# Steps 14 and 15 of a gated cross-attention kernel in a new order, with roundings, masks and weight loads moved

## The reference

```
x = x + tanh(g_xattn) * attention(layernorm(x), ctx, ctx)     # 16 heads of 16 channels, biases, output projection
x = x + tanh(g_ffn)   * moe(layernorm(x))

moe: t = rmsnorm(x) * norm_w
     probs = softmax(t @ gate_w.T); the two best of 8 experts, weights renormalised
     h1 = t @ w1.T + 2 * (t @ a1[e].T) @ b1[e].T ;  h3 likewise with w3, a3, b3      # F = 1024, rank 16
     act = silu(h1) * h3
     out_e = act @ w2.T + 2 * (act @ a2[e].T) @ b2[e].T ;  out = weighted sum of the two
```

## Time and profile before

| | |
|---|---|
| median of 3 runs | 507.66 us (506.61 to 508.35) |
| profiled execution, its own time | 509.6 us |
| its span, first to last instruction | 507.7 us |
| mean granted TensorE clock | 0.993 |
| TensorE busy | 487.7 us (96%) |
| VectorE busy | 357.9 us (70%) |
| ScalarE busy | 266.6 us (53%) |
| GpSimd busy | 282.4 us (56%) |

### The profile page before, as it was taken

One profiled execution on the slowest core, in us unless ns is written; L12 is line 12 of the kernel. 1 busy time (PEld: TensorE's weight loads), 2 busy tenths in 40 slices (PEclk: granted clock), 3 DMA queues, 4 the chain that ended last, 5 costly groups with the idle time before them and its releaser, 6 DMA issues.

```text
span 507.7 us, 11754 instructions
## 1 busy us (share of the span) xinstructions
PE 487.7 (96%) x4350; PEld 456.2 (90%) x4350; DVE 357.9 (70%) x768; ACT 266.6 (53%) x584; POOL 282.4 (56%) x339
## 2 busy tenths in 40 slices
PE   7888999999999999999899999999999999999996
PEld 6657999999999999997789999899999999999994
DVE  6866777877878877888577869856486456854444
ACT  4456766666676777667666533443335333233331
POOL 5645666666666666561676536644386444854440
PEclk9989999999999999999989999999999999999999
DMA  7793786677777777553601000010000100001001
GB/s 199 180 289 93 216 214 153 157 182 190 189 179 180 180 176 169 120 111 57 204 10 17 1 0 1 1 34 0 1 0 2 34 1 1 0 2 34 0 1 32
DMA packets 51144, 45.83 MB, mean 90 GB/s; under 512 B 33935, under 2 KB 40115, under 8 KB 51088
## 3 DMA queue, kind: packets, MB, share of 16 engines
q1 hardware_dynamic: 41310, 23.18, 19.6%
q0 software_dynamic: 7504, 18.69, 14.1%
q10 hardware_dynamic: 2274, 3.21, 2.0%
HBM read 20.59 MB, written 6.66 MB: 54 GB/s over the span
## 4 chain that ended last, share of the span: by engine, by line
PE 84%; DVE 6%; DMA 5%; issue 2%; ACT 2%; POOL 1%; ACTq 0%; DVEq 0%
PE bank L1368 14%; PE bank L1223 7%; PE bank L1246 7%; PE bank L1372 7%; PE bank L1385 6%; PE bank L1420 6%; PE bank L1205 6%; PE bank L1259 6%; PE bank L1193 5%; PE bank L1400 4%; DMA QS<-crow 3%; PE bank L1292 3%; PE bank L1403 2%; PE bank L1180 2%; PE bank L1335 2%
## 5 line engine op out<-in xcount | busy, mean ns | idle before, releaser
L970 DVE TENSOR_REDUCE nmax<-bank 100x1 f32<-100x361 f32 x256 | 130.0, 529 | 38.4 <-PE bank L1223 33.4
L419 POOL TENSOR_TENSOR awl<-hb,awh 128x400 fp32r<-128x400 f32 x63 | 70.2, 1114 | 109.4 <-ACT awh L627 109.4
L529 ACT ACTIVATE pt<-bank 120x400 f32<-120x400 f32 (+1 forms) x192 | 90.3, 503 | 25.8 <-PE bank L1246 12.2
L627 ACT ACTIVATE awh<-hb 128x400 fp32r<-128x400 f32 x64 | 34.5, 539 | 119.0 <-DVE hb L906 118.7
L1223 PE MATMUL bank<-KS,QS 96*100 96x362 f32 x256 | 86.9, 358 | 5.2 <-DVE nmax L970 4.8
L899 DVE TENSOR_TENSOR hb<-sil,bank 128x400 f32<-128x400 f32 x64 | 36.5, 570 | 73.7 <-PE bank L1385 37.9
L1246 PE MATMUL bank<-QS,KS 97*120 97x200 f32 (+1 forms) x384 | 66.4, 271 | 1.6 <-ACT pt L529 1.0
L1246 PEld LDWEIGHTS bank<-QS,KS 97*120 97x120 f32 (+1 forms) x384 | 60.2, 184 | 2.8 <-DMA QS<-crow 1.7
L328 POOL TENSOR_TENSOR cth<-craw,cth 128x724 fp32r<-128x724 f32 x16 | 27.7, 1729 | 63.0 <-ACT cth L475 54.8
L1223 PEld LDWEIGHTS bank<-KS,QS 96*100 96x100 f32 x256 | 41.6, 167 | 12.8 <-DVE nmax L970 7.3
L333 POOL DMA_DIRECT2D QS<-q_dram x90 | 46.0, 519 | 0.4 <-issue 0.3
(11 more groups left out here) (221 smaller groups left out, 1116.3 us busy)
## 6 DMA issues: line engine op xcount, KB each, us to landing
KS<-kn SPq DMA_DIRECT2D x128, 90.5 KB, 3.3
KS<-kn POOLq DMA_DIRECT2D x64, 90.5 KB, 3.4
craw<-ctxT POOLq DMA_DIRECT2D x14, 361.0 KB, 4.9
QS<-q_dram POOLq DMA_DIRECT2D x92, 50.0 KB, 3.6
q_dram<-qn ACTq DMA_DIRECT2D x4, 400.0 KB, 4.1
o_dram<-on SPq DMA_DIRECT2D x16, 100.0 KB
xr<-o_dram SPq DMA_DIRECT2D x16, 100.0 KB
y<-xs SPq DMA_DIRECT2D x8, 200.0 KB
```

The source lines that it names most:

```text
L419: nc.gpsimd.tensor_tensor(awl[:, g % 2, slot], hb[:, slot], awh[:, g % 2, slot].bitcast(F32), ALU.subtract).then_inc(m["p_awl"], 1)
L529: nc.scalar.activation(pt[0:TW[t], u, :], pT[u % 3][0:TW[t], 0:CS], ACT.Exp, scale=float(DH) ** -0.5).then_inc(m["act_e"], 1)
L970: nc.vector.tensor_reduce(nmax[:, h // 8, pos % 8:pos % 8 + 1], pS[h % 2][0:S, 0:T], AX.X, ALU.max, negate=True).then_inc(m["dve_s"], 1)
```

## The change

`body` now runs to step 13 only, and two orders written by hand follow: `late_step()` for step 14 and `last_step()` for step 15. On TensorE:

```diff
@@ body, end of the step
-                for u in range(UN):
+                if i == B - 3:
+                    s_head(B - 1, 0)
+                    s_head(B - 1, 1)
+                for u in range(UN // 2):
+                    pv_unit(i, u)
+                if i == B - 3:
+                    s_head(B - 1, 2)
+                    s_head(B - 1, 3)
+                for u in range(UN // 2, UN):
                     pv_unit(i, u)
                 second_rows(i + 1)
+            def late_step():
+                s_head(B - 1, 4)
+                st_unit(B - 2, 0)
+                s_head(B - 1, 5)
+                st_unit(B - 2, 1)
+                st_unit(B - 2, 2)
+                s_head(B - 1, 6)
+                o_turn(B - 2)
+                s_head(B - 1, 7)
+                token_turn(0, 0)
+                st_unit(B - 2, 3)
+                s_head(B - 1, 8)
+                s_head(B - 1, 9)
+                st_unit(B - 2, 4)
+                pe.wait_ge(m["dve_on"], B - 2)
+                row_turn(B - 1, 0)
+                st_unit(B - 2, 5)
+                s_head(B - 1, 10)
+                st_unit(B - 2, 6)
+                s_head(B - 1, 11)
+                st_unit(B - 2, 7)
+                on_turn(B - 2)
+                token_turn(0, 1)
+                st_unit(B - 2, 8)
+                s_head(B - 1, 12)
+                st_unit(B - 2, 9)
+                s_head(B - 1, 13)
+                st_unit(B - 2, 10)
+                y_proj(B - 2)
+                s_head(B - 1, 14)
+                s_head(B - 1, 15)
+                st_unit(B - 2, 11)
+                for u in range(UN):
+                    pv_unit(B - 2, u)
+                second_rows(B - 1)
+            def last_step():
+                gate(0)
+                o_turn(B - 1)
+                st_unit(B - 1, 0)
+                st_unit(B - 1, 1)
+                u_half(0, 0)
+                st_unit(B - 1, 2)
+                st_unit(B - 1, 3)
+                on_turn(B - 1)
+                u_half(0, 1)
+                st_unit(B - 1, 4)
+                st_unit(B - 1, 5)
+                st_unit(B - 1, 6)
+                y_proj(B - 1)
+                st_unit(B - 1, 7)
+                st_unit(B - 1, 8)
+                index_turn(0)
+                st_unit(B - 1, 9)
+                st_unit(B - 1, 10)
+                st_unit(B - 1, 11)
+                for u in range(UN):
+                    pv_unit(B - 1, u)
+                weight_turn(0)
```

`u_half(n, a)` is one half of `u_proj(n)`. `weight_turn(0)` waits for `d_ul` in place of `d_mk`. On ScalarE the roundings and `normed_x(0, k)` stand at the head of the late step, and `normed_x(1, k)` moves to groups 0 and 1:

```diff
+            def late_step():
+                w_high(0)
+                w_high(1)
+                for k in range(4):
+                    normed_x(0, k)
+                w_high(2)
+                row_copy(B - 2, 1)
+                (wait; copy of osb)
+                expo(B - 2, 0)
+                row_send(B - 2, 1)
+                expo(B - 2, 1), expo(B - 2, 2), tokens_high(0, 0), expo(B - 2, 3), expo(B - 2, 4)
+                row_copy(B - 1, 0), expo(B - 2, 5), expo(B - 2, 6), expo(B - 2, 7), w_high(3)
+                expo(B - 2, 8), w_high(4), tokens_high(0, 1), expo(B - 2, 9) to expo(B - 2, 11)
+                row_send(B - 1, 0), w_high(5)
+            def last_step():
+                row_copy(B - 1, 1), (wait; copy of osb), row_send(B - 1, 1), w_high(6)
+                expo(B - 1, 0) to expo(B - 1, 3), u_high(0, 0), u_high(0, 1)
+                expo(B - 1, 4) to expo(B - 1, 9), halves_of_weight(0), expo(B - 1, 10), expo(B - 1, 11)
+                nc.scalar.activation(warm_s[:], nmr[:, 0:1], ACT.Silu)
@@ groups
-                if more and f < 2 and c:
+                if more and f < 2:
                     normed_x(c + 1, 2 * f)
                     normed_x(c + 1, 2 * f + 1)
```

(In this block the one-call lines are joined by commas.) On VectorE, GpSimd and SyncE:

```diff
@@ VectorE, body
+                if i == 11: root(0, 0) to root(0, 2) ahead of head 14, root(0, 3) to root(0, 6) at the end
+                if i == 12: root(0, 7) to root(0, 9) ahead of head 14, root(0, 10) to root(0, 12) at the end
@@ VectorE, late_step: heads 0, 1, first_sum(B - 3), heads 2 to 6, shares(B - 2), head 7, quotient(B - 2),
@@   heads 8, 9, tokens_low(0, 0), heads 10, 11, turned_o(B - 2), heads 12, 13, variance(10), first_sum(B - 2),
@@   heads 14, 15, tokens_low(0, 1), variance(11)
+            def last_step():
+                logits(0)
+                shares(B - 1)
+                quotient(B - 1)
+                best_two(0)
+                turned_o(B - 1)
+                u_low(0, 0)
+                u_low(0, 1)
+                first_sum(B - 1)
+                variance(12)
+                masks(0)
+                first_u(0, 0)
+                second(0)
+                first_u(0, 1)
+                weights_of_two(0)
+                second_u(0, 0)
+                second_u(0, 1)
+                variance(13)
@@ VectorE, groups 0 and 1: turned_o(B + g) between gated(g, 1) and weighted(g, 1), no longer after summed(g)
@@ GpSimd
-                if 2 <= i < B:
+                if 2 <= i <= B - 3:
                     ...
-                    for b in range(i - 2, B if i == B - 1 else i - 1):
+                    for b in range(i - 2, B if i == B - 3 else i - 1):
                         (xs[:, b, :] += tbh)
@@ GpSimd, i == B - 2: w_low(0) to w_low(6) in a row; second(0), second_u(0, 0), second_u(0, 1) are gone
@@ SyncE
                 body(i)
-                if i == B - 2:
+                if i == B - 1:
                     for dst, src in second_halves:
                         sp.dma_start(dst, src).then_inc(m["fw2_in"], 16)
```

More of the change, by code:

```diff
@@ L430, in _ @@
                     w_low(2)
-                if i == B - 1:
                     w_low(3)
                     w_low(4)
[L434 to L438, removed]
+                    w_low(5)
+                    w_low(6)
             for g in range(NC * FT):
@@ L1051, in body @@
                 head(i + 1, 12)
-                if i == B - 2:
-                    tokens_low(0, 1)
                 head(i + 1, 13)
+                if i == 11:
+                    for k in range(3):
+                        root(0, k)
+                if i == 12:
+                    for k in range(7, 10):
+                        root(0, k)
                 head(i + 1, 14)
@@ L1069, in body @@
                         root(0, k)
-                if i == 11:
-                    root(0, 6)
-            def last_step(i):
+                if i == 12:
+                    for k in range(10, 13):
+                        root(0, k)
+            def late_step():
+                head(B - 1, 0)
+                head(B - 1, 1)
+                first_sum(B - 3)
+                head(B - 1, 2)
+                head(B - 1, 3)
+                head(B - 1, 4)
+                head(B - 1, 5)
+                head(B - 1, 6)
+                shares(B - 2)
+                head(B - 1, 7)
+                quotient(B - 2)
+                head(B - 1, 8)
+                head(B - 1, 9)
+                tokens_low(0, 0)
+                head(B - 1, 10)
+                head(B - 1, 11)
+                turned_o(B - 2)
+                head(B - 1, 12)
+                head(B - 1, 13)
+                variance(10)
+                first_sum(B - 2)
+                head(B - 1, 14)
+                head(B - 1, 15)
+                tokens_low(0, 1)
+                variance(11)
@@ L1114, in _ @@
                 gated(g, 1)
+                if g < 2:
+                    turned_o(B + g)
                 weighted(g, 1)
@@ L1325, in gate, with u_half @@
                 last.then_inc(m["pe_g"], 1)
-            def u_proj(n):
[L1328 to L1337, removed]
+            def u_half(n, a):
+                if n == 0:
+                    if a == 0:
+                        pe.wait_ge(m["d_ttl"], 2)
+                        pe.wait_ge(m["p_w"], 1)
+                        pe.wait_ge(m["dve_s"], H * B)
+                    else:
+                        pe.wait_ge(m["act_c"], 2 * B)
+                elif a:
+                    pe.wait_ge(m["d_lg"], n + 1)
+                for t, (hw, hc) in enumerate(TERMS):
+                    for j in range(KT):
+                        last = mm(bU[n][a][:, 0:CS], agw[hw][:, j, E_ + a * ER:E_ + (a + 1) * ER],
+                                  tt[hc][n % 2][:, j, :], start=t + j == 0, stop=t + j == 3)
+                last.then_inc(m["pe_u"], 1)
+            def u_proj(n):
+                u_half(n, 0)
+                u_half(n, 1)
             def index_turn(n):
```

221 lines of the change are left out of this document (96 added, 125 removed).

## The result

| | before | changed |
|---|---|---|
| median | 507.68 us (4 runs, 506.61 to 508.35) | 503.4 us (4 runs, 502.57 to 504.5) |
| ratio of the runs | | 0.9919, 95% interval 0.9893 to 0.9945 |
| profiled execution, its own time | 509.6 us | 504.5 us |
| its span | 507.7 us | 502.6 us |
| mean granted clock | 0.993 | 0.991 |

The kernel became 4.3 us faster; 6.0 were forecast. The measured time lies within the range given.

A forecast was written before the change was run, and what follows sets the result against it. The loose stretch from step 13's first pv_unit to up held 22.8 us of work in 30.47, the rest waits or slow clock. Gains 1.0 + 6.1 less 0.3 and 0.8 made 6.0 us: 501.7 us, range 499.6 to 504.8.

The forecast's parts named there:

- (a) roots: Steps 11 and 12: three of seven small VectorE operations moved ahead of head 14, into its idle time; gain 1.0 us.
- (b) steps 14 and 15: New order of heads and ScalarE's work: gate 2.4 us earlier, up at 254.85 instead of 260.93; gain 6.1 us.
- 1.7 the clock: Step 15: part of the 6.1 us gain, from the granted clock no longer falling to 0.50 before up.
- the 22.8 us of work: TensorE's counted work from step 13's first pv_unit to up, of 30.47 us; the other 7.6 were waits or slow clock.
- (c) masks: Start of the feed-forward part: VectorE gains three operations, four products take 3.7 us with GpSimd idle; delta(0,0) and delta(0,1) level.
- (d) normed_x: ScalarE's four normed_x(1, k) move into groups 0 and 1; loss 0.3 us, between 0 and 1.0.
- (e) GpSimd: Five additions in step 13 delay k_stack_low(15), free with 1.6 us in hand; w_low(0) to (6) cost nothing.
- (f) the loads: Six second weight halves behind body(15) land at 262.1, wanted by w_high(7) at 263.5; free, row sends no longer meet them.
- (g) hand-offs: TensorE exactly in time at a dozen places of the walk; four charged 0.2 us each, loss 0.8 us.
- no fall of the clock: Rival, steps 14 and 15: TensorE thins out and runs at half clock again, giving 503.9 us; chance 0.14.
- no wait for the products: Rival, hand-over to feed-forward: products take 1.77 instead of 0.99, delta(0,0) waits 2.6 us more, giving 504.3 us; chance 0.07.
- ScalarE never last: Rival, step 14: early heads cost TensorE what they save VectorE and ScalarE ends last; gain 3.8 us, 503.9; chance 0.08.

The follow-up runs named there:

- before again: The kernel before, unchanged, profiled and timed a second time; ratio 1.0006 to the kernel before.
- heads in pairs: Changed kernel with step 15's first two heads behind pv_unit 3 of step 13 and the next two behind pv_unit 8; 500.96 us, ratio 0.9867.
- masks run: Changed kernel with chunk 0's second masks back on GpSimd and the roundings w_low(5), w_low(6) behind them; 503.91 us, ratio 0.9921.
- loads early: Changed kernel with the second weight halves loaded behind step 14 again, as before the change; 503.98 us, ratio 0.9926.
- no early heads: Changed kernel with the first four heads of step 15 all behind the pv_units of step 13; 502.54 us, ratio 0.9929 to the kernel before.

## Why the prediction was right, point by point

**(a) roots.** Forecast 1.0 us, measured 1.1, added alone or taken away.

**(b) steps 14 and 15.** The walk gave 24.4 us from the pv_units of step 13 to up; the profile has 24.65. The gate was to gain 2.4 and gained 2.3: it stands 16.0 us after the first pv_unit of step 13 in both executions of before, and 13.67 after the same point (230.98) now. From the gate to up it is 10.98 us against the 13.20 of before again, 2.2 less; that execution waited 1.1 us for pt and 1.0 for the row send there, and the changed kernel waits for nothing. Two terms were off in size. One is "1.7 the clock", counted as gain: a fall did cost 1.6, but it is there in two of six profiles of the old order, so it is worth 0.5 on their average. Against the undisturbed 29.2 us the stretch gained 4.5 us, not 6.1; one execution was taken for all. The other is the 22.8 us of work: in the version with heads in pairs TensorE does the same list without a gap in 23.98, so 1.2 of the 7.6 us put down to waits and clock were work. The walk itself, not this count, made the forecast. The sum is then 1.1 + 4.5 = 5.6 from the start of step 12 to up (56.85 against 51.2), and 6.1 with the falls on their average.

**(c) masks.** The four products took 0.99 each, no wait for delta(0,0) beyond hand-offs. The products fell from 1.77 and 2.67 us to 0.99 once GpSimd was idle. dm took 1.21 us, to the end of w_low(6), and cost nothing, as forecast. By the rule of the Trainium skill (SBUF — State Buffer, "SBUF: two separate sides"), that the two engines lock each other out for whole instructions, the traces agree in both. The masks run shows what the part protects: 2.1 us of its stretch, 1.5 us of the median (503.91 against 502.37).

**(d) normed_x.** 0.3 us of loss were forecast, none is there: 246.97 and 246.90 us of feed-forward part against 246.84 and 247.11. No run puts the four back into the changed kernel, so what their move is worth there is not shown.

**(e) GpSimd.** k_stack_low(15) was issued at 226.41, behind five additions of 3.49 us in all; no head waited for KS. But "w_low(0) to (6): nothing" was wrong as a part: in the old place they hold up `weighted` as soon as up comes earlier.

**(f) the loads.** That they land in time was right. That their move costs and brings nothing was not: with the loads in the old place the changed kernel lost 3.7 us in the profiled execution (2.1 by the send, 1.6 by the clock); the medians of that set differ by 1.6 us (503.98 against 502.37). My own number for the row send, 3.9 us at most, came from a send that had met no weight loads; among or just behind them it took 6.01 and 6.17.

**(g) hand-offs.** 0.8 us were charged; the walk was short by 0.25. These 0.55 us charged too much, and the 0.3 of (d), made up for part of the clock term; that the forecast of 6.0 lies so near the 5.6 to 6.1 of the stretches is in part luck.

**The rivals.** None came about in the changed kernel: no fall of the clock in either profile between step 12 and up, no wait for the products, ScalarE never last, w_high(7) never behind a DMA.

**The total.** 5.6 to 6.1 us from the stretches stand against 4.3 and 5.1 in the two timings. In the profiles the rest lies ahead of step 12, whose start varies between 199.98 and 204.43 (203.66 and 201.59 for two kernels that differ from before only behind it), in good part with the early falls of the clock. The first profile of the changed kernel has the latest start of all. For the executions without a profile, which make the medians, this is inferred and not shown. Why the clock falls in one execution and not in the next was not tested. Nor was the new order of TensorE and ScalarE tried by itself, without the masks, loads and roots: that it carries most of the gain is read from the waits that are gone.

## What to carry to other kernels

A loss read from one profile may be that execution's own: before it is counted as gain, look for it in a second one, above all a stretch at half clock. Masks and loads showed nothing alone (each 1.00), yet taken back from the changed kernel they cost 2.1 and 3.7 us of a stretch: parts that show nothing alone may still let another part's gain through, because work that was hidden by a wait stands on the path once the wait is gone. And when the total scatters more than the effect, time the stretch between two marks of the program.

## What the runs showed of the hardware

A 3.1 KB transfer issued among six weight loads of 2.3 MB in all, or just behind them, took 6.01 and 6.17 us to release TensorE. In the attention steps ahead, where K and Q are loaded too, the sends that TensorE waited for took 5.2 to 5.9 us; one of step 14 was used 3.9 us after its issue without a wait. A head (362 columns) set among the small pv matmuls cost 0.44 us of TensorE's time instead of 0.17. The granted clock fell to 0.50 soon after a 1.9 us wait (loads early) and after two microseconds with 0.62 and 0.49 us of matmuls (no early heads, 230 to 232), but in the old order only twice in six executions with much the same waits. Each of these falls cost 1.5 or 1.6 us.
